# Mixture-of-experts layer on one core: GpSimd's gathers of the expert results issued three a quad

## The reference

```
x = x + attention(layernorm(x), ctx)
y = layernorm(x)                                   # T = 4096 tokens, H = 128
shared = silu(y @ sg.T) * (y @ su.T) @ sd.T
scores = sigmoid(y @ gate.T) + bias                # 64 experts in 8 groups, best 4 groups, top 6
topk_w, topk_i = lax.top_k(masked_scores, 6);  topk_w /= topk_w.sum() + 1e-08
h      = silu(y @ eg[e].T) * (y @ eu[e].T)         # 64 inner channels, for each expert e
routed = sum over the 6 chosen e of  topk_w * (h @ ed[e].T)
out    = x + shared + routed
```

## Time and profile before

| | us |
|---|---|
| median of 3 runs (lowest, highest) | 871.64 (868.51, 877.1) |
| span of the profiled execution | 860.9 |
| first silu of the experts' stage | 398.2 |
| first gather | 456.8 |
| last silu (quad 63) | 818.4 |
| last gather issued | 851.9 |

### The profile page before, as it was taken

How to read it: one execution, slowest core, us unless ns; L and a number is a source line. 1 busy time by engine, 2 the same in 40 slices (tenths; PEclk the granted TensorE clock), 3 DMA queues, 4 the chain that set the end, 5 groups by cost and what they waited for, 6 DMA issues and landing times.

```text
span 860.9 us, 12037 instructions
## 1 busy us (share of the span) xinstructions
PE 515.8 (60%) x3204; PEld 433.7 (50%) x3204; DVE 453.8 (53%) x2264; ACT 355.5 (41%) x962; POOL 389.5 (45%) x425
## 2 busy tenths in 40 slices
PE   3877655554356654315897567476876767665700
PEld 2545443332234432205896567475775767665700
DVE  6486666555565756564153444365464654243452
ACT  3464433443433532212283454355554554234400
POOL 2006555555555565565205434343435435444464
PEclk9985555556755555556698676687868687778765
DMA  7333222222222232242363333244434444444231
GB/s 219 139 124 105 96 93 69 71 84 95 99 99 99 93 102 99 96 149 64 105 163 99 92 96 100 76 123 105 111 104 111 113 127 120 126 115 107 74 98 49
DMA packets 98708, 90.60 MB, mean 105 GB/s; under 512 B 10576, under 2 KB 85456, under 8 KB 98640
## 3 DMA queue, kind: packets, MB, share of 16 engines
q1 hardware_dynamic: 85232, 64.26, 25.3%
q0 software_dynamic: 12288, 25.29, 10.6%
q10 hardware_dynamic: 1120, 0.28, 0.1%
HBM read 41.32 MB, written 48.46 MB: 104 GB/s over the span
## 4 chain that ended last, share of the span: by engine, by line
PE 26%; issue 25%; POOL 22%; another core or an unknown queue 13%; ACT 9%; DVE 4%; ACTq 1%; POOLq 0%; DMA 0%; DVEq 0%
POOL pages L445 17%; PE bank_s L1141 14%; PE bank_q L1141 4%; PE bank_s L1137 3%; ACT d_now L497 2%; PE bank_o L1141 2%; ACT gu_now L497 2%; POOL rstd L435 2%; ACT pxt L497 1%; POOL p_t L478 1%; PE bank_r L1141 1%; ACTq L497 1%; POOL empty L478 1%; PE bank_w L1141 1%
## 5 line engine op out<-in xcount | busy, mean ns | idle before, releaser
L1141 PE MATMUL bank_s<-pxt,gu_now 128*128 128x64 f32 x768 | 124.7, 331 | 96.5 <-ACT pxt L497 75.0
L1141 PEld LDWEIGHTS bank_s<-pxt,gu_now 128*128 128x128 f32 x768 | 120.4, 246 | 101.7 <-ACT pxt L497 79.4
L478 POOL DMA_INDIRECT p_t<-results,place_i x96 | 91.2, 950 | 149.6 <-DVE xb L1081 69.6
L1097 DVE TENSOR_TENSOR h_t<-bank_s,s_act 64x256 f32<-64x256 f32 x128 | 54.7, 427 | 185.6 <-ACT s_act L658 107.0
L478 POOL DMA_INDIRECT empty<-results,place_i x96 | 90.9, 947 | 105.1 <-DVE xb L1081 58.6
L445 POOL DMA_INDIRECT pages<-payload,place_i x96 | 93.1, 970 | 38.5 <-issue 27.4
L445 POOL DMA_INDIRECT pages<-payload_b,place_i x96 | 93.1, 970 | 35.2 <-issue 26.4
L658 ACT ACTIVATE s_act<-bank_s 64x512 f32<-64x512 f32 x64 | 37.8, 591 | 132.1 <-remote 86.2
L435 POOL TENSOR_TENSOR rstd<-ve,minus_half 128x4 f32<-128x4 f32 (+1 forms) x21 | 18.5, 882 | 134.0 <-DVE ve L913 131.2
L519 ACT ACTIVATE p_t<-bank_s 128x512 f32<-128x512 f32 x64 | 36.1, 598 | 65.5 <-issue 26.9
L1241 PE MATMUL bank_o<-bias_h,row_h 96*128 96x256 bf16 x16 | 6.2, 388 | 76.1 <-ACT o_t L497 74.1
(11 more groups left out here) (169 smaller groups left out, 1164.6 us busy)
## 6 DMA issues: line engine op xcount, KB each, us to landing
pg<-pages SPq DMA_DIRECT2D x64, 258.0 KB
results<-y_s SPq DMA_DIRECT2D x64, 256.0 KB
pages<-empty SPq DMA_DIRECT2D x21, 774.0 KB
w_gu<-in_expert_gu SPq DMA_DIRECT2D x16, 256.0 KB
w_d<-in_expert_d SPq DMA_DIRECT2D x31, 128.0 KB
out_x<-xb SPq DMA_DIRECT2D x16, 128.0 KB
xb<-in_x SPq DMA_DIRECT2D x3, 512.0 KB, 7.9
pages<-payload,place_i POOLq DMA_INDIRECT x96
```

The costliest lines, as they stand in the source:

```text
L478: pool.indirect_dma_start(out=ys[n % YS_SLOTS][:, k, :], out_offset=None, in_=results[0:landed * QUAD * P, :], in_offset=bass.IndirectOffs ...
L1097: dve.tensor_tensor(h_t[q % 2][h * INTER:(h + 1) * INTER, :, h, :], gu_ps[q % 2][INTER:2 * INTER, :].rearrange("p (g h t) -> p g h t", g=Q ...
L1141: return pe.matmul(dst, w, v, start=True, stop=True)
```

## The change

In front of each of the first 165 gathers (tile 0 to the middle of tile 27) GpSimd waits for one event. The gathers are numbered through, with an offset of 27; number divided by three gives the quad, the remainder the event: the quad's silu (`act_ready`), its product h (`h_ready`), or the copy of the previous quad's result (`y_ready`). So tile n belongs to quads 9 + 2n and 10 + 2n, three gathers each. The waits that were there stay in front of each tile. Tiles 28 to 31 and the last three gathers of tile 27 have no event.

```diff
+GATHERS_A_QUAD = TOPK // 2
+FIRST_BEAT = FIRST_SUM - 6
...
+            def beat(step):
+
+                q, part = divmod(step, GATHERS_A_QUAD)
+                if part == 0:
+                    pool.wait_ge(act_ready, q + 1)
+                elif part == 1:
+                    pool.wait_ge(h_ready, HALVES * (q + 1))
+                else:
+                    pool.wait_ge(y_ready, q)
+
             def gather(n):
...
                 for k in range(TOPK):
+                    if GATHERS_A_QUAD * FIRST_BEAT + TOPK * n + k < GATHERS_A_QUAD * NQ:
+                        beat(GATHERS_A_QUAD * FIRST_BEAT + TOPK * n + k)
                     pool.indirect_dma_start(out=ys[n % YS_SLOTS][:, k, :], out_offset=None, in_=results[0:landed * QUAD * P, :],
```

## The result

The changed kernel takes 797.76 us (794.14 to 801.73, 4 runs), the kernel before in the same measurement 871.24 (868.51 to 877.1): a ratio of 0.920, 95% interval [0.913, 0.927]. After the change the silu is L672, the gathers L492, TensorE's product L1155, its transpose L1151, ScalarE's copy L511.

A forecast was written before the change was run, and what follows sets the result against it. Bound: TensorE's updates held 1.43 us per gather in a run. Span 860.9 - 10.2 (before quad 21) - 66.7 (quads 21 to 62) + 3.8 (tail) = 787.8, plus 10.7 to the median: 798.5, said as 799 us; range 758 to 840.

The forecast's parts named there:

- The price, 1.43 us a gather: In gather runs: each gather takes 1.43 us of something TensorE's updates need; updates wait for multiples of it; chance 50%.
- Rival E: Quads 21 to 62: the hold is a fixed price per run, 8.0 us a quad, 923 us in all; chance 8%.
- the gathers then aren't the cause: Rival reading of late TensorE updates: gathers don't hold them, only the tail changes, 875 us, same; chance 7%.
- A quad, 5.2 us: Quads 21 to 62: 4.56 us to the release plus 0.59 and 0.02; 42 quads take 218 us, minus 67.
- never in the cases I read before the third: In gather runs: a held TensorE update got out after a gather, never before the third in the cases read.
- rival C: Quads 21 to 62: runs of three hold nothing or to 2.86 us; 4.3 us a quad, 761 us; chance 14%.
- rival B: Quads 21 to 62: the hold outlasts three served gathers; 5.9 us a quad, 828 us; chance 18%.
- threes that merge into longer runs: Gathers from quad 19 should stand in threes; if these merged into longer runs, the forecast would be wrong.
- The clock, near 0.95: Quads 21 to 62: TensorE never idle for 3 us, so the granted clock stays near 0.95, above 0.9.
- The run-in, minus 10.2: Quads 12 to 20: nine gathers hold 12.9 us, then shorter runs; quad 21 starts at 523.1 instead of 533.3 us.
- The tail, plus 3.8: After the last silu: the 24 last gathers start 8.4 us after it starts instead of 4.60, 3.8 us more.
- From span to median, plus 10.7: Whole kernel: the earlier median, 871.64, lay 10.7 us above the profiled span; that difference was added to the forecast span.

The follow-up runs named there:

- the second run: The changed kernel, unaltered, measured once more in another set where updates are late: 799.34 us beside 867.51, a ratio of 0.925.

## Why the prediction was right, step by step
**The price, 1.43 us a gather, paid by TensorE's updates at whole multiples: held, with exceptions.** Updates came after 2, 3, 4, 6, 8 and 12 gathers (2.86, 4.33, 5.69, 8.53, 11.43, 17.07 us from the first), and it is gone with the gathers (667.64 us) and with their indirect form (676.53). Rival E, a fixed price for a run, falls with the runs of three. The exceptions are half multiples: of ScalarE's 217 waits for "remote" over 0.2 us in the gathers' time of the six held traces with six gathers a tile, 27 end near a half, counted from the first gather of a run. The longest wait of the kernel before is one, to 497.75, 16.42 us or 11.5 x 1.43 from its run's first gather at 481.33; the prediction calls each long wait that was followed a multiple. So something finer than whole gathers counts too, and no run says what. The rule of the Trainium skill, "SBUF — State Buffer", section "Who interferes with whom", that TensorE and ScalarE wait on nobody: the held runs differ, by 362.9 against 196.0 us for the same 51 quads with six gathers a tile and with one; the free runs agree with it. The rule speaks of ports of the on-chip memory, and no run here shows what the late updates wait for. The measurement decides on what I drew from it, that the gathers then aren't the cause: they are.

**A quad, 5.2 us: 5.32 measured (5.37 in the second run), 223.5 us for 218.** The mean was right, its shape wasn't. I forecast an even 5.2; only 19 of 42 quads lie near it. The rule built on "never in the cases I read before the third" failed: rival C's release at the second gap happens (2.86 us), and so does a form of rival B, since a run that starts as the former is being served counts on from it (5.81 us and a quad of 7.0). The prediction itself named threes that merge into longer runs as a sign that it is wrong, and thirteen times they did; it also expected more "remote" waits, and there were fewer. The short and the long quads nearly cancel, which no step of the sum could know; that the mean fell so near 5.2 is partly luck.

**The clock, near 0.95: wrong, 0.83 and 0.86.** I reasoned that TensorE would never be idle for 3 us, but merged runs leave such stops, and the work behind them stands at the lower clock:

```profile
714.31 3.68 PE L1155 MATMUL bank_s<-pxt,gu_now 128*128 128x64 f32 x16 [3.68 <-ACT pxt L511]
```

The mean lies between the levels of 1.2 and 2.4 GHz still: TensorE is busy 184.56/42 = 4.39 us a quad, where one gather a tile, at clock 1.00, needs 183.27/51 = 3.59. That it cost little, since the hold and not TensorE's work is what most quads wait for, is my reading; no run tests it.

**The run-in, minus 10.2: minus 9.0.** The nine gathers held as written, 12.94 us or 9 x 1.44 (in the second run 12.12, a half multiple). From quad 16 to 21 the quads together took 30.1 us for 28.9, not each its own: the one in which the six start took 7.9 for 9.4, the next 6.9 for 5.2. TensorE's stretch still stood at a clock of 0.75.

**The tail, plus 3.8: plus 4.5.** The 24 gathers start 9.05 us after the last silu starts, not 8.4. The term that I mis-sized: the first gather of a tile has two waits before it (the buffer's and the event's) and starts 0.75 us after the silu's end (746.76 - 745.42 - 0.59), not the 0.27 of a gather with one; the rest are two of the six that take 1.33 and 1.39 us instead of 1.25. The same half microsecond stands in the quads that begin a tile (600.53 - 599.78 = 0.75, against 605.72 - 605.45 = 0.27 in the next). The kernel before has it too: its even tiles, with the wait for `y_out` ahead, start 0.77 to 0.80 us after the adds, its odd ones 0.27. The run at 562.60 of the earlier trace rows starts 0.79 us after adds that end at 561.81; the prediction took its 0.27 from the other, an odd tile.

**From span to median, plus 10.7: wrong in kind.** A run's device time is its span and 1.7 us more (794.14 against 792.4). The kernel before was profiled in a quick run (860.9 + 1.7 = 862.6, under the lowest of the others), and I carried its luck as a constant. The profiled run of after is also below its median, by 3.6 us. The sum's span of 787.8 was 4.6 too low, the difference carried (10.7 where it was 797.76 - 792.4 = 5.4) 5.3 too high; that the median came within 1.3 of the forecast is owed to both.

**DMA, 140 GB/s: 138.** No bound, as said.

## What to carry to other kernels
When an engine's updates come late, measure from the first instruction of whatever runs beside it: a lateness in multiples of one number names a suspect before any experiment. Where GpSimd's indirect DMAs hold updates, what one run costs is what sticks out from under the work beside it, so split runs below that length, and look for what could pile them up again (data that lands late, a buffer that comes free late); fewer indirect DMAs, or plain ones, brought more than any order of them that was tried (667.64 and 676.53 us against 799.34), in kernels that left work out or read other rows. Read a single profiled run's distance from the median as spread until other kernels show it to be constant.

## What the runs showed of the hardware
- The same kernel before takes 595 or 850 to 871 us, and what the traces of the two levels show to differ is whether TensorE's updates are held: at the free level the change is worth nothing (0.998 to 1.000 for its variants), at the held level 7.5 to 8%. I had not expected that a gain of this size hangs on it. Even before the first gather the held level costs some 94 us. The first stage has GpSimd's scatters, also indirect, and in the kernel before its late updates stand on the same multiples (timeline):

```profile
74.28 1.03 POOL L445 DMA_INDIRECT pages<-payload,place_i  x1 [0.20 <-issue]
...
87.17 0.28 ACT L532 ACTIVATE sig<-bank_r 128x128 f32<-128x128 f32 x1 [2.26 <-remote]
...
91.47 0.47 ACT L505 ACTIVATE q_t<-bank_q,bqs_s 128x256 f32<-128x256 f32 x1 [4.03 <-remote]
```

  12.89 and 17.19 us from the first scatter are 9 and 12 x 1.43. At the free level the first stage has no wait for "remote" and the same work (TensorE busy 216.4 us against 216.8). That the scatters cause the 94 us wasn't tried by taking them out.
- ScalarE's update was not late in the middle of a run: VectorE starts its product 0.03 us after the silu's end (609.19 against 609.16).
- At the held level an indirect DMA of 128 rows holds TensorE's updates for 1.43 us whether it moves 64 KB or 16; 64 KB by a plain transfer from GpSimd don't. Its issue costs GpSimd 0.95 us against 0.55. With one gather a tile, the held level costs quads 12 to 62 nothing (196.0 and 195.9 us).
- At the free level GpSimd's queue becomes the bound: 192 gathers x 1.25 = 240 us. With one a tile the kernel takes 563.14 us, with plain transfers 565.11.
